# Feed-forward up and gate products by one level of Strassen, in four PSUM banks

## What is computed

```
def ternary_quant(w):
    scale = jnp.mean(jnp.abs(w)) + EPS
    q = jnp.clip(jnp.round(w / scale), -1.0, 1.0) * scale
    return w + jax.lax.stop_gradient(q - w)

wu, wg, wd = ternary_quant(W_up), ternary_quant(W_gate), ternary_quant(W_down)
up = jnp.einsum('bsd,ed->bse', x, wu)          # 512 -> 2048
gate = jnp.einsum('bsd,ed->bse', x, wg)        # 512 -> 2048
hidden = jax.nn.silu(up) * gate
return jnp.einsum('bse,de->bsd', hidden, wd)   # 2048 -> 512

x = x + _L0_ffn_ref(_layernorm(x, axis=-1), L0_ffn_W_up, L0_ffn_W_gate, L0_ffn_W_down)
```

## Time and profile before

| | |
|---|---|
| median of three runs | 746.62 us |
| the profiled execution | 747.43 us |
| its span in the profile | 745.7 us |
| granted TensorE clock, mean | 0.991 of 2.4 GHz |
| TensorE, VectorE, ScalarE, GpSimd busy | 715.1, 377.0, 273.2, 125.0 us |
| feed-forward stage, first to last matmul | 403.5 to 739.4 us |

### The profile page before, as it was taken

How to read it: one execution, slowest core, us unless ns; L and a number is a source line. 1 busy time by engine, 2 the same in 40 slices (tenths; PEclk the granted TensorE clock), 3 DMA queues, 4 the chain that set the end, 5 groups by cost and what they waited for, 6 DMA issues and landing times.

```text
span 745.7 us, 11582 instructions
## 1 busy us (share of the span) xinstructions
PE 715.1 (96%) x3979; PEld 380.9 (51%) x4008; DVE 377.0 (51%) x622; ACT 273.2 (37%) x426; POOL 125.0 (17%) x186
## 2 busy tenths in 40 slices
PE   8999999999999988999998999999999999999996
PEld 5556557557565655666544444444444444444442
DVE  5667766866856654664464343353434433342233
ACT  4365545536537243344222322222222222222221
POOL 3113624314315600000010000020000200020002
PEclk8999999999999999999999999999999999999999
DMA  8914026025127289531011000020001200010001
GB/s 226 367 59 168 1 113 208 18 94 204 41 114 282 89 298 334 198 113 30 15 30 30 14 15 14 1 71 14 14 14 15 70 14 14 14 56 1 0 1 56
DMA packets 45606, 64.00 MB, mean 86 GB/s; under 512 B 22784, under 2 KB 22784, under 8 KB 44544
## 3 DMA queue, kind: packets, MB, share of 16 engines
q1 hardware_dynamic: 41728, 50.89, 21.7%
q0 software_dynamic: 3840, 12.59, 4.5%
HBM read 46.69 MB, written 12.59 MB: 79 GB/s over the span
## 4 chain that ended last, share of the span: by engine, by line
PE 79%; DVE 7%; DMA 4%; issue 3%; ACT 3%; POOL 2%; SPq 1%; POOLq 0%; DVEq 0%; ACTq 0%
PE bank L1340 29%; PE bank L1070 26%; PE bank L1350 13%; PE bank L1063 4%; DVE region L761 2%; PE bank L1227 2%; PE bank L1263 2%; PE bank L1241 2%; DMA n<-sorted_tokens 2%; DVE late L757 1%; DMA sorted_residual<-rows,pos 1%; DMA w_att<-nrm 1%; DMA stage<-in_L_attn_Wv_dram 1%; SPq L188 1%; POOL sorted_residual L324 1%
## 5 line engine op out<-in xcount | busy, mean ns | idle before, releaser
L1340 PE MATMUL bank<-w_att,region 128*128 128x512 f16 (+1 forms) x1024 | 231.1, 379 | 2.7 <-DMA w_att<-nrm 2.7
L1340 PEld LDWEIGHTS bank<-w_att,region 128*128 (+1 forms) x1024 | 100.1, 98 | 123.7 <-issue 3.4
L1033 DVE SCALAR_TENSOR_TENSOR tmp<-tmp,hk,bank 128x512 f32<-128x512 f32 x64 | 47.8, 747 | 155.9 <-PE bank L1340 155.5
L1350 PE MATMUL bank<-region,tmpA 128*128 (+1 forms) x452 | 111.3, 379 | 1.5
L1070 PE MATMUL bank<-late,w_att 128*128 128x512 f16 x384 | 87.2, 383 | 1.1 <-DVE region L804 1.0
L609 ACT ACTIVATE tmp<-bank,qs 128x512 f32<-128x512 f32 x64 | 44.0, 687 | 116.7 <-PE bank L1340 116.7
L307 POOL TENSOR_SCALAR ve<-mv 128x1 f32<-128x1 f32 (+1 forms) x37 | 9.2, 248 | 455.8 <-DVE mv L971 340.5
L616 ACT ACTIVATE tmpA<-tmp 128x512 f16<-128x512 f32 x62 | 39.0, 629 | 120.2 <-DVE tmp L1033 120.2
L1350 PEld LDWEIGHTS bank<-region,tmpA 128*128 128x128 f16 x480 | 46.8, 98 | 56.8 <-DVE stage L1017 0.9
L1037 DVE TENSOR_TENSOR tmpA<-tmp,tmpA 128x512 f16<-128x512 f32 x62 | 43.0, 693 | 44.1 <-ACT tmpA L616 44.1
L1070 PEld LDWEIGHTS bank<-late,w_att 128*128 128x128 f16 x384 | 37.6, 99 | 44.1 <-DVE region L804 2.0
(11 more groups left out here) (144 smaller groups left out, 809.7 us busy)
## 6 DMA issues: line engine op xcount, KB each, us to landing
stage<-in_L_ffn_W_up_dram SPq DMA_DIRECT2D x8, 1024.0 KB, 5.9
stage<-in_L_ffn_W_gate_dram SPq DMA_DIRECT2D x8, 1024.0 KB, 5.3
rows<-sorted_residual SPq DMA_DIRECT2D x4, 1026.0 KB, 10.1
stage<-in_ctx_dram SPq DMA_DIRECT2D x4, 1024.0 KB, 6.6
stage<-in_L_ffn_W_down_dram SPq DMA_DIRECT2D x4, 1024.0 KB, 7.2
nrm<-in_L_ffn_W_down_dram SPq DMA_DIRECT2D x4, 1024.0 KB, 7.3
n<-sorted_tokens SPq DMA_DIRECT2D x16, 256.0 KB, 5.1
rows<-in_x_dram SPq DMA_DIRECT2D x1, 3072.0 KB, 19.3
```

The costliest lines, as they stand in the source:

```text
L1033: dve.scalar_tensor_tensor(out=h32, in0=sil, scalar=hk[:, 0:1], in1=gate_ps[:, :], op0=ALU.mult, op1=ALU.mult).then_inc(s["hid_mul"], 1)
L1340: mm = pe.matmul(dst, w[:, bass.ds(cf_c, 1), k * P:(k + 1) * P].rearrange("p a n -> p (a n)"), x3T[:, bass.ds(b, 1), i, k].rearrange("p a ...
L1350: mm = pe.matmul(ffy_ps[t][:, :], hid[:, parity, i, t * P:(t + 1) * P], tern[2][:, bass.ds(c, 1)].rearrange("p a n -> p (a n)"), start=(st ...
```

## The change

The up product of two blocks of 128 features (2t and 2t+1 of the upper half, the same two of the lower half) with 512 tokens is a product of a 2 x 2 block matrix: the features in two halves, the model width in two halves, the tokens in two halves of 256 (tiles p and p + 2). One level of Strassen's scheme in Winograd's form makes it by seven products in place of eight. The four differences and sums of weight blocks, S1 to S4, are made once, for up on VectorE and for gate on GpSimd, from expert step 10 on. Those of the tokens are made for each batch, in two parts of 2 tiles each (`x3_sums`): seven quarters of 256 elements, 1792 in all, whose high parts ScalarE copies and whose remainders GpSimd subtracts, each followed by a transposing DMA of its own. Each product is 8 matmuls of 256 columns into one of four rotating banks. VectorE adds a product out of its bank to sums held in SBUF (the first one ScalarE copies), so that after seven products four results of 128 x 512 stand there; the same for gate; then silu, the gated product on VectorE, its high part on ScalarE and its remainder on GpSimd. `down` is unchanged in its number of matmuls; its four blocks of a group stand among the next group's products. All 16 groups are written out without a loop. Output rows are collected in the first expert's weights.

The core of the diff, engine by engine (SyncE, GpSimd, ScalarE, VectorE, TensorE):

```diff
+        def x3_turned(b, p):
+            for h in range(2):
+                sp.wait_ge(s["x3_lo" if h else "x3_hi"], 2 * b + p + 1)
+                sp.dma_start_transpose(out=x3S_in[b % 2][:, h, :, p * P:(p + 1) * P], in_=x3h[:, h]).then_inc(
+                    s["x3_lo_in" if h else "x3_hi_in"], 16)
...
+        def x3_lo(k):
+            pool.wait_ge(s["x3_hi"], k + 1)
+            if k > 0:
+                pool.wait_ge(s["x3_lo_in"], 16 * k)
+            pool.tensor_tensor(x3h[:, 1], x3_flat[:, 0:7 * H], x3h[:, 0], ALU.subtract).then_inc(s["x3_lo"], 1)
...
+        third_rsqrt(0)
+        third_rsqrt(1)
+        pool.wait_ge(s["unit_copy"], 12 * T)
+        gate_sum(S1[1], A21[1], A22[1], ALU.add, 0)
+        x3_lo(0)
+        gate_sum(S3[1], A11[1], A21[1], ALU.subtract, 1)
+        gate_sum(S2[1], S1[1], A11[1], ALU.subtract, 2)
+        x3_lo(1)
+        gate_sum(S4[1], A12[1], S2[1], ALU.subtract, 3)
+
+        def group(b, t):
+            n = T * b + t
+            if n < NT - 1:
+                hid_lo(n, 0, 0, g11)
+                hid_lo(n, 1, 3, g22)
+            if b + 1 < B and t % 2 == 0:
+                third_rsqrt(2 * b + 2 + t // 2)
+            if b + 1 < B and t % 2 == 1:
+                x3_lo(2 * b + 2 + t // 2)
+            if n < NT - 1:
+                hid_lo(n, 2, 1, g21)
+                hid_lo(n, 3, 2, g12)
+            if t == 0 and b > 0:
+                send_out(b - 1)
...
+            act.activation(g22, wk_ps[(14 * n + 7) % 4][:, :], ACT.Copy).then_inc(s["gate_copy"], 1)
+            hid_hi(n, 0, 0, g11)
+            if b + 1 < B and t % 2 == 1:
+                x3_hi(2 * b + 2 + t // 2)
+            hid_hi(n, 1, 3, g22)
+            hid_hi(n, 2, 1, g21)
...
+            if i in (10, 13):
+                x3_normalise((i - 10) // 3)
+            if i in (11, 14):
+                x3_sums((i - 11) // 3)
...
+            if i in (8, 9):
+                dve.wait_ge(s["y_evac"], i)
+                x3_stats(i - 8)
+            if i == 10:
+                dve.wait_ge(s["unit_copy"], 12 * T)
+                up_sum(S1[0], A21[0], A22[0], ALU.add, 0)
+            if i == 12:
+                up_sum(S3[0], A11[0], A21[0], ALU.subtract, 1)
+            if i == 15:
+                up_sum(S2[0], S1[0], A11[0], ALU.subtract, 2)
+            if i == 16:
+                up_sum(S4[0], A12[0], S2[0], ALU.subtract, 3)
...
+            def gate_of(out, m, other):
+                dve.wait_ge(s["gate_mm"], 7 * n + m + 1)
+                dve.tensor_tensor(out, wk_ps[(14 * n + 7 + m) % 4][:, :], other, ALU.add).then_inc(s["gate_add"], 1)
...
+            gate_of(g22, 4, g21)
+            gate_of(g12, 4, g12)
...
+            dve.wait_ge(s["gate_add"], 7 * n + 4)
+            gate_of(g21, 5, g21)
+            gated(n, 1, u22, g22)
+            dve.wait_ge(s["gate_add"], 7 * n + 5)
+            gate_of(g12, 6, g12)
+            dve.wait_ge(s["gate_add"], 7 * n + 6)
+            gated(n, 2, u21, g21)
...
+            dve.wait_ge(s["gate_add"], 7 * n + 7)
+            gated(n, 3, u12, g12)
...
-        def two_pass(dst, w, cf_c, b):
...
+        def part(bank, w, c, slot, m):
+
+            for q in range(2):
+                for h in range(2):
+                    for k in range(2):
+                        mm = pe.matmul(wk_ps[bank][:, q * H:(q + 1) * H], w[:, c + q, k * P:(k + 1) * P],
+                                       x3S_part[slot][:, h, m, k], start=(h == 0 and k == 0), stop=(h == 1 and k == 1))
             return mm
...
+            up(0, A11, 0)
+            up(1, S2, 5)
+            if n == 0:
+                second(STEPS - 1)
+            up(2, A12, 1)
+            up(3, S3, 4)
+            downs_before(0)
+            up(4, S1, 3)
+            up(5, A22, 6)
+            up(6, S4, 2)
+            downs_before(1)
+            gate(0, A11, 0)
+            gate(1, S2, 5)
+            gate(2, A12, 1)
+            gate(3, S3, 4)
+            downs_before(2)
+            gate(4, S1, 3)
+            gate(5, A22, 6)
+            gate(6, S4, 2)
+            downs_before(3)
+
+        pe.wait_ge(s["up_sums"], 4)
+        pe.wait_ge(s["gate_sums"], 4)
+        for b in range(B):
+            pe.wait_ge(s["x3_hi_in"], 32 * b + 32)
+            pe.wait_ge(s["x3_lo_in"], 32 * b + 32)
             for t in range(T):
-                for i in range(2):
...
+                group(b, t)
```

More of the change, by code:

```diff
@@ L602, in _ @@
             expert_step(i)
[L604 to L630, removed]
+        def silu(n, q, dst, src):
+            act.activation(dst, src, ACT.Silu, scale=qs[:, 0:1]).then_inc(s["up_act"], 1)
@@ L633, in _ @@
+        for b in range(B):
+            for t in range(T):
+                group(b, t)
+        hid_hi(NT - 1, 3, 2, g12)
     @block.vector
@@ L1058, in _ @@
+        for b in range(B):
+            for t in range(T):
+                group(b, t)
+        finish(B - 1, range(T), [4 * NT - 3 + i for i in range(T)])
     @block.tensor
@@ new lines, in down, with downs @@
+        def down(c, u, tiles, begins, ends):
+            for t in tiles:
+                for q in range(2):
+                    for h in range(2):
+                        mm = pe.matmul(ffy_ps[t][:, :], hid[:, u, h, q, (t % 2) * P:(t % 2 + 1) * P], tern[2][:, c + q],
+                                       start=(begins and q == 0 and h == 0), stop=(ends and q == 1 and h == 1))
+            return mm
+        def downs(n, i):
+            t, b = n % T, n // T
+            u, c, tiles, lo = ((0, 2 * t, (0, 1), 1), (1, C // 2 + 2 * t, (0, 1), 3),
+                               (3, C // 2 + 2 * t, (2, 3), 2), (2, 2 * t, (2, 3), 4))[i]
+            pe.wait_ge(s["hid_lo"], 4 * n + lo)
+            if t == 0 and i % 2 == 0:
+                if b > 0:
+                    pe.wait_ge(s["out_made"], T * (b - 1) + i + 2)
+                else:
+                    pe.wait_ge(s["y_evac"], STEPS)
+            down(c, u, tiles, t == 0 and i % 2 == 0, t == T - 1 and i % 2 == 1).then_inc(s["down_mm"], 1)
@@ new lines, in _ @@
+        pe.wait_ge(s["up_sums"], 4)
+        pe.wait_ge(s["gate_sums"], 4)
+        for b in range(B):
+            pe.wait_ge(s["x3_hi_in"], 32 * b + 32)
+            pe.wait_ge(s["x3_lo_in"], 32 * b + 32)
+            for t in range(T):
+                group(b, t)
+        c = C // 2 - 2
+        for t, (first, then) in enumerate((((0, 1), (1, 3)), ((0, 1), (1, 3)), ((3, 3), (2, 4)), ((3, 3), (2, 4)))):
+            for u, lo in (first, then):
+                pe.wait_ge(s["hid_lo"], 4 * NT - 4 + lo)
+                mm = down(c + C // 2 if u in (1, 3) else c, u, (t,), False, u == then[0])
+            mm.then_inc(s["down_mm"], 1)
```

323 lines of the change are left out of this document (179 added, 144 removed).

## The result

The changed kernel takes **760.5 us** (median of 4 runs, 760.0 to 761.0) where the kernel before takes 746.9 (4 runs of the same comparison): 1.0179 times as long, interval 1.0162 to 1.0197. The forecast was 765, range 751 to 778, slower with a chance of 0.90. The profiled execution of the changed kernel took 760.04 us, its span is 758.1 (before: 747.43 and 745.7).

The account below looks back on a forecast made before the run. TensorE, busy 96% of the span, was taken to bound the kernel. On 747.43 us, -25.3 (matmuls) + 36.6 (batch starts) + 5.6 (expert steps) + 1.7 (end) gave 766.0; the runs' median lies 0.8 below, so 765 us, range 751 to 778.

Parts of the forecast that it names:

- The matmuls: Feed-forward groups on TensorE: 256-column matmuls cost 109.3 ns, a group 19.15 us; sixteen groups save 25.3 us (20.5 to 27.6).
- The rival of no saving: Feed-forward products: half-width matmuls don't cost half; at no saving at all 790 us, chance 0.08.
- VectorE inside a group: Feed-forward groups: VectorE's sums and gated products take 11.2 us of 19.15, nothing waits inside a group, cost nothing.
- The batch start: Three later batch starts: TensorE waits 10.5 us for the second remainder's transpose, plus 1.7 of clock; 36.6 us in all.
- The walk through the group: One feed-forward group timed with T = 0 at its first up product; TensorE resumes at T = 29.7 instead of 19.15.
- The expert steps: Weight sums and first batch's quarter sums moved into steps 8 to 16: net +5.6 us (-3.6 to +10.5).
- The four meetings with GpSimd: VectorE instructions blocked by GpSimd sums: normalisations in steps 10 (1.65) and 13 (2.1), sums after 12 (1.9) and 15 (2.75 us).
- The end: After the last group four tiles wait 2.3 us for the third quarter's `hid_lo`, against gaps of 0.6: +1.7 us.
- the port isn't held for long instructions: VectorE beside GpSimd: expert steps lose nothing (-3.6), each batch start stalls 9.3 us; 752 us, chance 0.14.
- the remainder is there in time: Batch starts: TensorE's wait, priced at 12.2 us each, costs nothing; 728.6 us, chance 0.08.

Follow-up runs that it names:

- the second experiment: Changed kernel with GpSimd making the late remainder ahead of the first two `hid_lo` in each batch's fourth group: 749.1 us, 1.0042 of the kernel before.
- The first experiment: Changed kernel with both halves of the next batch's normalised rows made one group earlier: 727.3 us, 0.9738 of the kernel before.
- the third: Changed kernel with 160 unread matmuls of 128 columns on TensorE before the wait at each later batch start: 754.9 us, 1.0108 of the kernel before.
- the first five experiments: Changed kernel with halves earlier 727.3, late remainder first 749.1, dummy matmuls 754.9, gate sums on VectorE 759.8, the last plus transposes one step later 759.1 us.

## Why the prediction was right

The sign, the place and the mechanism held; the sum was 18.6 us on the profiled execution against 12.4 measured (13.6 between the medians). Of the 6.2 us, 3.0 are the expert steps, 2.1 the batch starts and 1.6 the spread of executions ahead of step 10; the end cost 0.4 more than forecast. Step by step:

- **The matmuls** were forecast at 109.3 ns and a saving of 25.3 us. Measured: 109.2 ns, groups of 19.14, 25.4 us. Interpolating between two neighbours of the trace was enough. With the stalls gone and two smaller losses mended the kernel takes 0.9665 of the time of the kernel before, so this saving was there all along. The rival of no saving is out.
- **VectorE inside a group** was costed at nothing, and TensorE waits nowhere inside one.
- **The batch start** was forecast at 10.5 us of stall and 1.7 of clock, 36.6 in all; measured 9.5 and 2.0, 34.5. The walk through the group gave the remainder's end at T = 25.5 and TensorE's start at 29.7; counted from that group's first product (457.67) they came at 24.7 and 28.8. The order of the walk held, each step a little short of its forecast: `hid_lo` ended at T = 20.7 (20.9), VectorE's gated product behind it at 21.3 (21.6). The remainder's 4.01 us begin at 20.7 and hold some 0.4 in which that gated product still ran; alone it takes 3.58, as the second experiment shows (forecast 3.9). The transposing DMA took 4.0 (4.2). The first experiment showed that the late second half is the cause, the second that GpSimd's order makes 4 of the 9.5 us of stall, the third what part of the loss is clock.
- **The expert steps** are the term that failed in size: +5.6 forecast, +2.6 measured. The four meetings with GpSimd were forecast to cost 8.4 us (1.65, 1.9, 2.75, 2.1). Three did (1.3, 3.6, 1.8); at the fourth VectorE's sum started 0.14 us before GpSimd's and took 1.26 us, unblocked. Of the blocks only about 2.1 us net reached the path. A second cost was not foreseen at all: the longer transposing DMAs hold up the step's register reads. In the changed kernel six reads of steps 13 and 16 and of the products behind them take 0.58 to 1.04 us in place of 0.30, and TensorE stands idle 1.10, 1.47 and 0.36 us before three products; in the kernel before no read from step 10 on takes over 0.31.
- **The end**: +1.7 forecast, +2.1 measured, but by other parts. The forecast set a wait of 2.3 us against gaps of 0.6. Measured are a wait of 2.1, against 1.7 of waits in the whole stage before, and 1.7 us of slow matmuls that the forecast didn't have. That the sums agree is luck.
- The rival that **the port isn't held for long instructions** is out: 4.77 in place of 1.21 us beside a sum of 4.07, and 3.41 in place of 0.74 beside a remainder of 3.58. SBUF — State Buffer (the Trainium skill, section Who interferes with whom) says that the lock lasts for the whole instruction; over 4 us these rows agree. VectorE: DVE Perf Modes (the Trainium skill, section on N = 2048 bf16) gives 1.22 us for a sum of 2048 two-byte values; VectorE's took 1.21 to 1.26 when unblocked. The prediction had taken 1.8.
- The rival that **the remainder is there in time** was priced at 728.6. The experiment that makes it so took 727.3; by the measured terms of the expert steps the price would have been 725.6, so part of the nearness is luck.

## What to carry to other kernels

When a change replaces short instructions by a long one, look at what stands ahead of it in its own engine's order and who waits for its end: here one 4 us instruction, with the work that feeds it, turned 25 us of saved matmul into 14 us of loss when placed in the last group of four, and into 19 us of gain one group earlier. The three long stalls of TensorE were paid twice, by waiting and by a low clock behind them, and dummy matmuls over the wait gave back the second part only. And a sequencer that reads a register right before it is needed belongs to the path. What reading it ahead gives depends on what the read then meets: 6.6 us behind the change, 1.7 in the kernel before.

## What the runs showed of the hardware that was not expected

- A read of a number from SBUF into TensorE's registers takes 0.30 us, and up to 1.04 beside a transposing DMA of 14 blocks (0.73 beside one of 8). Two reads right before a product cost TensorE nothing in steps 10 and 11, some 0.35 us a step in the steps with the weight units, and 1.4 to 1.5 us beside the transfers.
- VectorE's normalisation, which reads one fp32 tensor, is held up by GpSimd's long sums too: three instructions 2.49 and 3.00 us beside them, 1.19 without. The prediction had counted on it; no row of the kernel before showed it.
- After the same wait of 2.10 us at the end, TensorE ran on at half speed in the changed kernel (0.43 us a matmul of 512 columns, for some 3 us) and at full speed in the first five experiments. The long stalls ahead don't decide it: two of the five, those with the gate sums on VectorE, had the same three of 9.5 us. What does, no run here shows. Nor does a shorter stall lose less clock: behind 5.4 to 5.6 us the first 32 matmuls took 5.35, 6.00 and 6.45 us, behind 9.5 us 4.98, 5.57 and 5.88.
